# First self attention of a six-layer decoder kernel: eight batches in turn, or one chain of steps over all heads

## The chip, the cores and the metric

The kernel runs on one core of a Trainium2 chip, as one program. The metric is the device time in microseconds of one execution. TensorE is the matrix engine, VectorE and ScalarE read its results in PSUM, POOL (GpSimd) works on SBUF, and SyncE issues the transfers. Each engine takes its own instructions in program order and waits on semaphores.

## What is computed

A decoder of six layers over x of 8 batches x 256 tokens x 512, each followed by an addition and a layer normalization. Only the first, a causal self attention with 16 heads of width 128, is touched:

```python
q = (x @ Wq.T).reshape(b, n, H, D)              # H = 16, D = 128
kv = x @ Wkv.T                                  # one key part, one value part
kv_head = x @ Wkvh.T                            # one factor per head for k and v
g = x @ Wg.T
log_f_cumsum = cumsum([0, log_sigmoid(g)])[:-1]
kv_head = cumsum(kv_head * exp(log_f_cumsum))   # both over the tokens
k, v = kp x kh per head, vp x vh per head
q, k = rope(q), rope(k)
p = softmax(causal(q k^T / sqrt(D)))
x = layernorm(x + (p v) @ Wout.T)
```

## The kernel before

Float32 accuracy is kept by splitting: every operand of a product is a float16 high part and a float16 rest, and `three` (L114 to L116) issues three matmuls for one product. ScalarE rounds a PSUM bank to the high part, VectorE subtracts it from the bank for the rest; the pair is called hi and lo in the code.

`attn0` (from L316) loads and splits the weights, then goes through the eight batches one after the other. For each batch it first makes everything and then runs the heads:

- **x**: turned by TensorE (`turn_x`, L248) near the end of the batch before; `x_high` L255 on ScalarE, `x_low` L263 on VectorE.
- **Keys and values**: 24 matmuls of width 256 into the two S banks; ScalarE copies the values (L555), VectorE forms their rest and the rotated key (L631 to L636).
- **Gates**: 24 matmuls of width 256 into an O bank; ScalarE Abs, Exp, Ln (L558 to L562), VectorE two scans (L644, L648), between them ScalarE's Exp (L564). Their result is turned (L480) and copied (L673): one factor per token and head.
- **Queries**: eight products j of 12 matmuls of width 512 in the P banks. VectorE multiplies each with the rotation tables (L663, L664, L666), waits for itself and sets a semaphore by a small memset (L670), POOL adds the two parts (L421), TensorE turns four blocks (`turn`, L442), ScalarE and VectorE split them (L569, L623).
- **Keys per head**: POOL multiplies the rotated key with the factors (L411), eight times, TensorE turns (L442), ScalarE and VectorE split (L577, L623).
- **Heads**: a chain of 21 steps i. TensorE: scores of head i in one of two S banks (8 matmuls, the last of each half adds the mask, L503), turn of the probabilities (P) of head i-2, PV of head i-3 in one of two O banks, output product of head i-5 into the two P banks, which gather it over all heads. VectorE: row maxima (L690, L691), reciprocal (L698), rest of P (L704), rest of O (L711). ScalarE: P hi (L596), the exponentials (L585, L587, each with a read of the sum), O hi (L602). POOL weighs P with the reciprocals (L429, L431).
- **End**: VectorE adds x to the two output tiles (L285), measures (L288 to L291), POOL takes the root (L306), VectorE normalizes (L297).

PSUM has eight banks: two each of S, T (turned blocks), O and P. The order of the work is the program order of each engine's block; semaphores are counted per batch through `Counter` and `after`.

Of the kernel before, what the change touches and what calls it, by code (L numbers as in the profile page):

```python
# [7 lines left out]
F32 = mybir.dt.float32  # L8
F16 = mybir.dt.float16
# [7 lines left out]
P = 128  # L17
# [63 lines left out]
class Scope:  # L81
# [8 lines left out]
    def __exit__(self, *a):  # L90

        with self.nc.Block() as block:
# [223 lines left out]
def attn0(nc, G, W):  # L316
# [4 lines left out]
    NS = 2  # L321
    NPB = 3
    with Scope(nc, "a0", G.low) as sc:
# [10 lines left out]
        xT = [sc.sb(f"xT{i}", [P, KE, N], F16) for i in range(2)]  # L334
# [3 lines left out]
        v = [sc.sb(f"v{i}", [P, NT, D], F16) for i in range(2)]  # L338
        rope_q = sc.sb("rope_q", [P, 2, NT, D], F32)
        rope_k = sc.sb("rope_k", [P, 2, NT, D], F32)  # L340
        q_cos = sc.sb("q_cos", [P, 1, E], F32)
        q_sin = sc.sb("q_sin", [P, 1, E], F32)
        q_rot = sc.sb("q_rot", [P, 2, E], F32)
        k_part = sc.sb("k_part", [P, 2, D], F32)
        k_rot = sc.sb("k_rot", [P, NT, D], F32)
        kh_rows = sc.sb("kh_rows", [P, 1, H * D], F32)
# [5 lines left out]
        kvh_t = sc.sb("kvh_t", [P, NT, 2 * H], F32)  # L352
# [6 lines left out]
        NG = 8 + 8 + H  # L359
        G_Q, G_K, G_P = 0, 8, 16  # L360
        s = Names()
        x_counters(sc, s)
        s.t_ready = sc.counter("t_ready", NG)
        s.t_hi = sc.counter("t_hi", NG)
        s.t_lo = sc.counter("t_lo", NG)
        s.pr_ready = sc.counter("pr_ready", 2 + 8)
        s.pr_free = sc.counter("pr_free", 2 + 8)
        s.v_hi = sc.counter("v_hi", NT)
        s.gates_ready = sc.counter("gates_ready", 1)
        s.g_ln = sc.counter("g_ln", 3)  # L370
        s.g_sum = sc.counter("g_sum", 1)
        s.g_exp = sc.counter("g_exp", 1)
        s.kvh_ready = sc.counter("kvh_ready", 1)
        s.kvh_turned = sc.counter("kvh_turned", 1)
        s.kvh_t_ready = sc.counter("kvh_t_ready", 1)
        s.k_rot_ready = sc.counter("k_rot_ready", NT)
        s.kh_ready = sc.counter("kh_ready", 8)
        s.q_parts = sc.counter("q_parts", 8)
        s.q_ready = sc.counter("q_ready", 8)
        s.s_ready = sc.counter("s_ready", H)  # L380
        s.m_ready = sc.counter("m_ready", H)
        s.e_ready = sc.counter("e_ready", H)
        s.i_ready = sc.counter("i_ready", H)
        s.p_ready = sc.counter("p_ready", H)
        s.o_ready = sc.counter("o_ready", H)
        s.o_hi = sc.counter("o_hi", H)
        s.o_lo = sc.counter("o_lo", H)
        s.y_ready = sc.counter("y_ready", NT)
        s.chain = sc.counter("chain", NT * 1 + 2 + NT * LN_STEPS)
        ln_counters(sc, s)  # L390
        consts = sc.sem("consts")
        SB, Y = G.psS, G.psP

        with nc.Block() as block:
# [6 lines left out]
            @block.gpsimd  # L401
            def _(pool):
                for b in range(B):
                    def head_keys(j):

                        n, c = divmod(j, QC)
                        after(pool, s.kvh_t_ready, b, 1)
                        after(pool, s.k_rot_ready, b, n + 1)
                        if n:
                            after(pool, s.t_ready, b, G_K + c + 1)  # L410
                        pool.tensor_tensor(  # L411
                            kh_rows[:, 0, c * E:(c + 1) * E].rearrange("p (h d) -> p h d", h=HC),
                            k_rot[:, n:n + 1, :].broadcast_to([P, HC, D]),
                            kvh_t[:, n, c * HC:(c + 1) * HC].rearrange("p (h a) -> p h a", a=1)
                            .broadcast_to([P, HC, D]), ALU.mult).then_inc(s.kh_ready.handle, 1)

                    for j in range(8):
                        after(pool, s.q_parts, b, j + 1)
                        if j >= 2:
                            after(pool, s.t_ready, b, G_Q + j - 1)  # L420
                        pool.tensor_tensor(q_rot[:, j % 2, :], q_cos[:, 0, :], q_sin[:, 0, :], ALU.add)\  # L421
                            .then_inc(s.q_ready.handle, 1)
                        if j >= 5:
                            head_keys(j - 5)
                    for j in range(3, 8):
                        head_keys(j)
                    for h in range(H):
                        after(pool, s.i_ready, b, h + 1)
                        pool.tensor_tensor(prob[:, h % NPB, 0, 0:P], prob[:, h % NPB, 0, 0:P],  # L429
                                           inv[:, h % NPB, 0:1].broadcast_to([P, P]), ALU.mult)  # L430
                        pool.tensor_tensor(prob[:, h % NPB, 1, :], prob[:, h % NPB, 1, :],  # L431
                                           inv[:, h % NPB, 1:2].broadcast_to([P, N]), ALU.mult)\
                            .then_inc(s.p_ready.handle, 1)
                    for n in range(NT):
                        rstd_on_pool(pool, s, b, n, G)

            @block.tensor
            def _(pe):
                def turn(b, g, blocks):
                    after(pe, s.t_lo, b, g - 1)  # L440
                    for out, src in blocks:
                        last = pe.transpose(out, src, G.ident[:, :])  # L442
                    last.then_inc(s.t_ready.handle, 1)

                turn_x(pe, 0, s, G, G.psS)
                for b in range(B):
                    after(pe, s.x_lo, b, NT)
                    for n in range(NT):
                        for k in range(KE):
                            last = three(pe, G.psS[n][:, 0:2 * D], xT[0][:, k, n * P:(n + 1) * P],  # L450
                                         xT[1][:, k, n * P:(n + 1) * P], wkv[0][:, k, :], wkv[1][:, k, :],
                                         k == 0, k == KE - 1)
                        last.then_inc(s.pr_ready.handle, 1)
                    for i in range(2):
                        for k in range(KE):
                            last = three(pe, G.psO[0][0:2 * H, i * N:(i + 1) * N],
                                         wgh[0][:, k, i * 2 * H:(i + 1) * 2 * H], wgh[1][:, k, i * 2 * H:(i + 1) * 2 * H],
                                         xT[0][:, k, :], xT[1][:, k, :], k == 0, k == KE - 1)
                    last.then_inc(s.gates_ready.handle, 1)

                    def turn_q(j):
                        after(pe, s.q_ready, b, j + 1)
                        turn(b, G_Q + j, [(G.psT[j % 2][:, i * P:(i + 1) * P], q_rot[:, j % 2, i * P:(i + 1) * P])
                                          for i in range(HC)])

                    for j in range(8):
                        n, c = divmod(j, QC)
                        if j == 0:
                            after(pe, s.x_done, b, 0)
                        after(pe, s.pr_free, b, j + 1)  # L470
                        if j == 4:
                            after(pe, s.kvh_ready, b, 1)
                        for k in range(KE):
                            last = three(pe, G.psP[j % 2][:, :], xT[0][:, k, n * P:(n + 1) * P],
                                         xT[1][:, k, n * P:(n + 1) * P], wq[0][:, k, c * E:(c + 1) * E],
                                         wq[1][:, k, c * E:(c + 1) * E], k == 0, k == KE - 1)
                        last.then_inc(s.pr_ready.handle, 1)
                        if j == 4:
                            for n2 in range(NT):
                                last = pe.transpose(G.psO[1][:, n2 * 2 * H:(n2 + 1) * 2 * H],  # L480
                                                    kvh[:, n2 * P:(n2 + 1) * P], G.ident[0:2 * H, 0:2 * H])
                            last.then_inc(s.kvh_turned.handle, 1)
                        if j >= 2:
                            turn_q(j - 2)
                    turn_q(6)
                    turn_q(7)
                    for n in range(NT):
                        for c in range(QC):
# [5 lines left out]
                    def scores(h):  # L494
                        if h >= NS:
                            after(pe, s.e_ready, b, h - NS + 1)
# [2094 lines left out]
```

## Time and profile before

| What | Value |
|---|---|
| Time, median of 3 runs | 3481.63 us (3477.75 to 3481.8) |
| Profiled execution | 3481.1 us |
| Its span | 3479.1 us |
| PE busy in the span | 2910.5 us, 84% |
| VectorE, ScalarE, POOL busy | 2108.0, 1764.8, 1404.9 us |
| First self attention | 48.0 to 819.9 us of the span |

Times within the span are counted from its start. A busy PE includes matmuls that overlap in the pipeline, so the time of a group of matmuls is best read as the distance between starts. The granted clock is the share of 2.4 GHz: 1.00 is 2.4 GHz, 0.50 is 1.2 GHz, and a value between is a mean over time. A timeline's row gives start, duration, engine, line, operation, what it writes and reads, and how many consecutive ones are merged; the brackets tell how long the engine had been idle and what released it.

### The profile page before, as it was taken

Reading aid. Unit: us, or ns where it says so; the run is one execution under the profiler, and the core shown is the slowest. Engines: PE = TensorE matmul, PEld = TensorE weight load, DVE = VectorE, ACT = ScalarE, POOL = GpSimd, SP = SyncE. Lnnn points to the kernel's source line nnn. Section 1 sums busy time; section 2 is a strip of 40 time slices with the busy share of each in tenths; the row PEclk is TensorE's granted clock in tenths of the full one; section 3 lists DMA queues with packets and bytes.
Section 4 is the critical chain, followed back from the end, with each engine's and each line's share of the span. In section 5 each row is a group of like instructions: output and inputs, shape, how many; then the busy total and the mean of one; then the engine's idle time right before and its main releaser. Section 6 shows DMA issues by size and latency. Waiting matters only on the chain. (4 is left out here: it accounts for less than half of the span.)

```text
span 3479.1 us, 64422 instructions
## 1 busy us (share of the span) xinstructions
PE 2910.5 (84%) x24866; PEld 2050.9 (59%) x24866; DVE 2108.0 (61%) x4574; ACT 1764.8 (51%) x3865; POOL 1404.9 (40%) x1537
## 2 busy tenths in 40 slices
PE   4989889894888886699999978887999999975777
PEld 2566555552566664577777756665766666752333
DVE  4666666665677774555555446665555555555887
ACT  3444444443788886433333246664444444454775
POOL 1333343332587886244444424442122222213453
PEclk9988998987899997799999999998999999997898
DMA  4000000001000000300000001102011110022000
GB/s 159 1 1 1 1 1 1 1 1 64 1 2 2 2 2 20 135 1 13 1 1 1 1 34 38 32 2 67 2 37 37 37 37 1 1 73 67 12 19 25
DMA packets 41189, 81.49 MB, mean 23 GB/s; under 512 B 5683, under 2 KB 9781, under 8 KB 40758
## 3 DMA queue, kind: packets, MB, share of 16 engines
q1 hardware_dynamic: 40886, 77.38, 6.5%
q8 instruction: 199, 3.26, 0.4%
q14 instruction: 104, 0.85, 0.1%
HBM read 73.18 MB, written 4.19 MB: 22 GB/s over the span
## 5 line engine op out<-in xcount | busy, mean ns | idle before, releaser
L960 POOL TENSOR_TENSOR c_pT<-c_prob,c_pT 128x512 f16<-128x512 f32 x256 | 293.4, 1159 | 106.4 <-ACT c_pT L917 105.7
L1813 POOL TENSOR_TENSOR c_prob<-c_prob,c_inv 128x512 f32<-128x512 f32 x128 | 133.5, 1043 | 310.6 <-DVE c_inv L2037 310.6
L960 POOL TENSOR_TENSOR a_pT<-a_prob,a_pT 128x384 f16<-128x384 f32 x128 | 120.6, 945 | 189.5 <-ACT a_pT L917 189.1
L1151 ACT ACTIVATE c_prob<-psT 128x512 f32<-128x512 f32 x256 | 155.8, 609 | 70.0 <-PE psT L1082 56.0
L1232 DVE TENSOR_REDUCE c_peak<-psS 128x2 f32<-128x512 f32 x256 | 169.8, 683 | 20.7 <-PE psS L1063 17.4
L917 ACT CAST c_pT<-c_prob 128x512 f16<-128x512 f32 x256 | 159.7, 624 | 0.0
L421 POOL TENSOR_TENSOR a_q_rot<-a_q_cos,a_q_sin 128x512 f32<-128x512 f32 x64 | 81.0, 1265 | 192.0 <-DVE a_q_sin L666 192.0
L429 POOL TENSOR_TENSOR a_prob<-a_prob,a_inv 128x128 f32<-128x128 f32 x128 | 51.1, 399 | 256.7 <-DVE a_inv L698 256.7
L596 ACT ACTIVATE a_pT<-psT,a_kvh_t 128x256 f16<-128x256 f32 (+1 forms) x256 | 93.6, 416 | 105.0 <-PE psT L442 105.0
L1961 ACT CAST c_pT<-psT 128x512 f16<-128x512 f32 x128 | 74.8, 584 | 140.0 <-PE psT L1825 140.0
L1953 ACT ACTIVATE c_prob<-psS,c_negmax 128x256 f32<-128x256 f32 x256 | 119.2, 474 | 44.8 <-DVE c_negmax L2030 41.2
L1489 POOL TENSOR_TENSOR f_ch<-f_h,f_c 128x256 f32<-128x256 f32 x88 | 76.1, 865 | 147.6 <-DVE f_h L1682 147.6
L114 PE MATMUL psP<-a_wq,a_xT 128*128 128x512 f16 x320 | 121.4, 379 | 13.1 <-DVE junk L670 10.3
L306 POOL TENSOR_TENSOR ln_rstd<-ln_ve,minus_half 128x1 f32<-128x1 f32 x48 | 31.9, 665 | 247.2 <-DVE ln_ve L291 247.2
L704 DVE SCALAR_TENSOR_TENSOR a_pT<-psT,a_kvh_t,a_pT 128x256 f16<-128x256 f32 (+1 forms) x256 | 95.1, 413 | 59.6 <-ACT a_pT L596 59.4
L2165 POOL TENSOR_TENSOR f_hg<-f_h,f_g 128x512 f32<-128x512 f32 x64 | 81.4, 1271 | 119.2 <-DVE f_h L2370 119.2
L2211 PE MATMUL psS<-f_wq,f_xq 128*128 128x512 f16 x256 | 81.6, 477 | 56.1 <-DVE f_h L2370 49.7
L1687 DVE TENSOR_TENSOR f_chs<-f_ch,f_chs 128x768 f16<-128x768 f32 x88 | 107.3, 1220 | 33.0 <-ACT f_chs L1625 32.4
L1063 PE MATMUL psS<-c_kS,c_qS 128*128 128x256 f16 x512 | 105.2, 290 | 24.0 <-DVE c_peak L1232 21.3
L115 PE MATMUL psP<-a_wq,a_xT 128*128 128x512 f16 x320 | 121.3, 379 | 0.0
L116 PE MATMUL psP<-a_wq,a_xT 128*128 128x512 f16 x320 | 121.3, 379 | 0.0
L569 ACT CAST a_qT<-psT 128x512 f16<-128x512 f32 x64 | 36.7, 586 | 163.4 <-PE psT L442 163.4
(580 smaller groups left out, 11456.7 us busy)
## 6 DMA issues: line engine op xcount, KB each, us to landing
c_feed<-in_L_ffn_w1T SPq DMA_DIRECT2D x16, 512.0 KB, 3.6
c_feed<-in_L_ffn_w2T SPq DMA_DIRECT2D x16, 512.0 KB, 3.6
f_stage<-in_f_up_gateT SPq DMA_DIRECT2D x16, 352.0 KB, 8.0
x_all<-in_x SPq DMA_DIRECT2D x1, 4096.0 KB, 14.1
a_stage<-in_L_attn_WqT SPq DMA_DIRECT2D x8, 512.0 KB, 7.6
a_stage<-in_L_attn_WoutT SPq DMA_DIRECT2D x8, 512.0 KB, 10.0
a_feed<-in_L_xattn_Wq SPq DMA_DIRECT2D x8, 512.0 KB, 3.7
c_feed<-in_L_xattn_Wo SPq DMA_DIRECT2D x8, 512.0 KB, 3.9
```

The costliest lines, as they stand in the source:

```text
L114: pe.matmul(out, a_hi, b_hi, start=first, stop=False, skip_group_check=True)
L115: pe.matmul(out, a_hi, b_lo, start=False, stop=False, skip_group_check=True)
L116: return pe.matmul(out, a_lo, b_hi, start=False, stop=last, skip_group_check=True)
L704: last = dve.scalar_tensor_tensor(pT[1][:, r, m, m * P:N], T[:, m * N + m * P:(m + 1) * N], kvh_t[:, m, H + h:H + h + 1], pT[0][:, r, m, m ...
L917: copy(pT[0][:, c % NPH, :], prob[:, c % NPX, :]).then_inc(p_high(c)[0], 1)
L960: pool.tensor_tensor(pT[1][:, c % NPH, :], prob[:, c % NPX, :], pT[0][:, c % NPH, :], ALU.subtract)\
L1063: last = pe.matmul(S[:, first:first + w], qS[:, b % 2, h // HB, n * P:(n + 1) * P], kS[:, b % 2, k_of(h), 0:w], start=True, stop=not causa ...
L1151: act.activation(prob[:, c % NPX, :], ST[c % 2][:, 0:EW], ACT.Exp).then_inc(s.e_done, 1)
L1232: dve.tensor_reduce(peak[:, h, :], S, X_AXIS, ALU.max).then_inc(s.m_done, 1)
L1687: dve.tensor_tensor(chs[1][:, t % 2, :, :], ch[:, t % 2, :, :], chs[0][:, t % 2, :, :], ALU.subtract).then_inc(s.ch_lo.handle, 1)
L1813: pool.tensor_tensor(prob[:, h % NPB, :, :], prob[:, h % NPB, :, :], inv[:, h % NPB, :].rearrange("p (n a) -> p n a", a=1).broadcast_to([P ...
L1953: last = act.activation(prob[:, r, n, :], S[:, n * N:(n + 1) * N], ACT.Exp, bias=negmax[:, r, n:n + 1], accum_out=sums[:, r, n:n + 1])
```

## The change

The loop over batches with its two parts is replaced by one loop over steps t from -14 to 135. Step t begins head t of all 128 heads (batch t // 16). What the next batch needs is made in steps given relative to its first head, so that it lies within the steps of this one:

- x at -14 (both tiles), keys and values at -12, gates at -10, their turn at -6; ScalarE's and VectorE's later parts of the gates one to three steps after -10.
- Query products at -7, -5, -3, -1, 1, 3, 5, 7, each turned two steps later; keys turned at -4, -2, ..., 10. So queries and their turns fall on odd steps, the keys' turns on even ones. Both are made head group by head group (four heads), for both token tiles.
- Output products come in pairs, of heads t-6 and t-5, in even steps.
- Layer normalization: the sum with x 20 steps after the batch's first head, measuring at 21, normalizing at 22.
- Bank use: S and O now have one bank each (`S`, `O`); the other two (`XB`) take x, kv, gates, the gates' turn and the query products in turn. The turn banks T alternate over all turns (k, q and P). The P banks hold the output products only.
- xT, v, kvh_t, k_rot double in size (by batch parity), k_part holds both tiles; the gates are copied out of PSUM once (`g_raw`). The two memsets after the rotations (L639, L670) go. Semaphores count over the whole part.

The diff, cut to its core (the first loop over t is POOL's, the second TensorE's):

```diff
-    NS = 2
     NPB = 3
+    AT_X, AT_KV, AT_GATES, AT_KVH = (-14, -14), -12, -10, -6
+    AT_Q = (-7, -5, -3, -1, 1, 3, 5, 7)
+    AT_K = (-4, -2, 0, 2, 4, 6, 8, 10)
+    TURN_Q, TURN_P, PV, WO, NORM = 2, 2, 3, 5, 21
+    FIRST, LAST = AT_X[0], (B - 1) * H + NORM + 3
...
-        SB, Y = G.psS, G.psP
+        S, O, Y = G.psS[0], G.psO[0], G.psP
+        TB, XB = G.psT, [G.psS[1], G.psO[1]]
...
+                for t in range(FIRST, LAST):
+                    for b, j in due(t, AT_K, -1):
+                        head_keys(b, j)
+                    if head(t, 1) is not None:
+                        weigh(head(t, 1))
+                    for b, j in due(t, AT_Q):
+                        add_q(b, j)
+                    for b, n in due(t, (NORM, NORM)):
+                        rstd(b, n)
...
+                def turn(key, blocks):
+                    no = turn_no[key]
+                    if no >= 2:
+                        pe.wait_ge(s.t_lo, no - 1)
...
+                def scores(a):
+                    b, h = divmod(a, H)
+                    if a:
+                        pe.wait_ge(s.e_ready, a)
...
+                for t in range(FIRST, LAST):
+                    if head(t, 0) is not None:
+                        scores(head(t, 0))
+                    for b, j in due(t, AT_K):
+                        turn_k(b, j)
+                    for b, j in due(t, AT_Q, TURN_Q):
+                        turn_q(b, j)
+                    for lag in (WO + 1, WO):
+                        if t % 2 == 0 and head(t, lag) is not None:
+                            project(head(t, lag))
+                    if head(t, TURN_P) is not None:
+                        turn_p(head(t, TURN_P))
+                    for b, n in due(t, AT_X):
+                        turn_x(b, n)
+                    for b, _ in due(t, (AT_KV,)):
+                        keys_values(b)
+                    for b, _ in due(t, (AT_GATES,)):
+                        gates(b)
+                    for b, _ in due(t, (AT_KVH,)):
+                        turn_kvh(b)
+                    for b, j in due(t, AT_Q):
+                        queries(b, j)
+                    if head(t, PV) is not None:
+                        pv(head(t, PV))
```

ScalarE's order in a step: hi of the keys' and of the queries' turn, exponentials of head t, the gates' second Exp, P hi, x hi, value copy, the gates' Abs, Exp and Ln, O hi of head t-3. VectorE's: row maxima of head t, lo of the keys' and the queries' turn, reciprocal of head t-1, the gates' scans, P lo of head t-2, the sums with x, x lo, the key's rotation, the gates' copies, the rotation of the queries, O lo of head t-3, measuring, normalizing.

## Rows read from the trace of the kernel before

**Rows 1.** Busy windows of batch 3: window, length, busy us by engine, PEclk, DMA share, GB/s

```profile
372.00:385.00 13.00, 8.41 (x42) 6.43 (x43) 6.04 (x9) 5.17 (x9) 5.95 (x6) 0.63 0.00 1
335.00:431.00 96.00, 86.54 (x588) 57.31 (x586) 60.84 (x176) 44.10 (x139) 35.06 (x50) 0.91 0.00 1
```

**Rows 2.** The tile a_xT on VectorE: durations, first and last start

```profile
L263 DVE TENSOR_TENSOR a_xT<-psS,a_xT x16: 680/686/692, 48.0 to 717.3; 128x512 f16<-128x512 f32 x16
```

**Rows 3.** Timeline: first scores, and the last batch's normalization on VectorE

```profile
96.46 0.29 PE L114 MATMUL psS<-a_kT,a_qT 128*128 128x128 f16 x1 [1.40 <-DVE a_kT L623]
...
814.89 0.69 DVE L285 TENSOR_TENSOR ln_r<-psP,x_all 128x512 f32<-128x512 f32 x1 [2.41 <-PE psP L116]
...
819.35 0.55 DVE L297 TENSOR_SCALAR x_all<-ln_r,ln_mv,ln_rstd 128x512 f32<-128x512 f32 x1 [0.44 <-POOL ln_rstd L306]
```

**Rows 4.** Timeline of TensorE over one head of batch 3, first matmul of each group

```profile
400.20 0.22 PE L114 MATMUL psS<-a_kT,a_qT 128*128 128x128 f16 x1
...
400.81 0.50 PE L442 MATMUL psT<-ident,a_prob 128*128 128x128 f32 x3
...
401.14 0.27 PE L114 MATMUL psO<-a_pT,a_v 128*128 128x256 f16 x1
...
401.64 0.38 PE L114 MATMUL psP<-a_wo,a_qT 128*128 128x512 f16 x1
...
402.93 0.22 PE L114 MATMUL psS<-a_kT,a_qT 128*128 128x128 f16 x1
```

**Rows 5.** Timeline of TensorE in batch 7: kv, gates, turn of queries, query product

```profile
720.20 0.27 PE L114 MATMUL psS<-a_wkv,a_xT 128*128 128x256 f16 x1
...
722.91 0.28 PE L114 MATMUL psO<-a_xT,a_wgh 128*32 128x256 f16 x1
...
735.20 0.60 PE L442 MATMUL psT<-ident,a_q_rot 128*128 128x128 f32 x4
735.64 0.38 PE L114 MATMUL psP<-a_wq,a_xT 128*128 128x512 f16 x1
...
738.23 0.60 PE L442 MATMUL psT<-ident,a_q_rot 128*128 128x128 f32 x4
```

**Rows 6.** Timeline of VectorE, then of ScalarE, over the same head

```profile
400.44 0.42 DVE L711 TENSOR_TENSOR a_qT<-psO,a_qT 128x256 f16<-128x256 f32 x1 [0.32 <-ACT a_qT L602]
401.00 0.29 DVE L690 TENSOR_REDUCE a_negmax<-psS 128x1 f32<-128x128 f32 x1
401.21 0.41 DVE L691 TENSOR_REDUCE a_negmax<-psS 128x1 f32<-128x256 f32 x1
...
402.11 0.74 DVE L704 SCALAR_TENSOR_TENSOR a_pT<-psT,a_kvh_t,a_pT 128x256 f16<-128x256 f32 x2 [0.41 <-ACT a_pT L596]
...
401.34 0.73 ACT L596 ACTIVATE a_pT<-psT,a_kvh_t 128x256 f16<-128x256 f32 x2 [0.94 <-PE psT L442]
401.96 0.37 ACT L585 ACTIVATE a_prob<-psS,a_negmax 128x128 f32<-128x128 f32 x1
...
402.66 0.22 ACT L587 ACTIVATION_READ_ACCUMULATOR a_prob<-psS,a_negmax 128x1 f32 x1
```

**Rows 7.** Timeline of VectorE and POOL in a rotation of queries

```profile
366.35 0.69 DVE L663 TENSOR_TENSOR a_q_cos<-psP,a_rope_q 128x512 f32<-128x512 f32 x1 [0.72 <-POOL a_q_rot L421]
...
367.74 0.69 DVE L623 TENSOR_TENSOR a_qT<-psT,a_qT 128x512 f16<-128x512 f32 x1
...
364.98 1.26 POOL L421 TENSOR_TENSOR a_q_rot<-a_q_cos,a_q_sin 128x512 f32<-128x512 f32 x1 [1.89 <-DVE a_q_sin L666]
```

**Rows 8.** Timeline in the gates: last scan of batch 0, table load in batch 3

```profile
62.18 0.68 DVE L648 TENSOR_TENSOR_SCAN a_kvh<-ones,a_g_fac 32x256 f32<-32x256 f32 x1
...
344.70 1.28 ACT L562 ACT_TABLE_LOAD   x1
```

**Rows 9.** Busy windows of two later layers: columns as in rows 1

```profile
1110.00:1160.00 50.00, 42.48 (x573) 30.49 (x570) 35.89 (x71) 40.62 (x74) 41.46 (x40) 1.00 0.01 2
3274.00:3291.00 17.00, 13.73 (x72) 6.44 (x72) 14.65 (x31) 12.50 (x19) 9.05 (x9) 0.90 0.09 32
```

More of the change, by code:

```diff
@@ new lines, in attn0, with due, head, turns @@
+        s.chain = sc.sem("chain")
+        consts = sc.sem("consts")
+        def due(t, places, shift=0):
+            out = []
+            for i, at in enumerate(places):
+                b, rest = divmod(t - shift - at, H)
+                if rest == 0 and 0 <= b < B:
+                    out.append((b, i))
+            return out
+        def head(t, lag):
+            return t - lag if 0 <= t - lag < B * H else None
+        def turns(t):
+            out = [("k", b, i) for b, i in due(t, AT_K)] + [("q", b, i) for b, i in due(t, AT_Q, TURN_Q)]
+            if head(t, TURN_P) is not None:
+                out.append(("p", *divmod(head(t, TURN_P), H)))
+            return out
@@ L453, in _, with gates @@
-                        last.then_inc(s.pr_ready.handle, 1)
+                            last = three(pe, bank(key)[:, n * 2 * D:(n + 1) * 2 * D], xT[0][:, r, k, rows],
+                                         xT[1][:, r, k, rows], wkv[0][:, k, :], wkv[1][:, k, :], k == 0, k == KE - 1)
+                    last.then_inc(s.x_ready, 1)
+                def gates(b):
+                    key, r = ("gates", b, 0), b % 2
+                    make_free(key)
                     for i in range(2):
+                        at = slice(i * 2 * H, (i + 1) * 2 * H)
@@ L466, in _ @@
[L466 to L484, printed above, removed]
@@ L535, in _ @@
[L535 to L547 removed]
+                            last = three(pe, bank(key)[0:2 * H, i * N:(i + 1) * N], wgh[0][:, k, at], wgh[1][:, k, at],
+                                         xT[0][:, r, k, :], xT[1][:, r, k, :], k == 0, k == KE - 1)
@@ new lines, in gates, with turn_kvh, queries @@
+                    last.then_inc(s.x_ready, 1)
+                def turn_kvh(b):
+                    key = ("kvh", b, 0)
+                    pe.wait_ge(s.kvh_ready, b + 1)
+                    make_free(key)
+                    for n in range(NT):
+                        last = pe.transpose(bank(key)[:, n * 2 * H:(n + 1) * 2 * H], kvh[:, n * P:(n + 1) * P],
+                                            G.ident[0:2 * H, 0:2 * H])
+                    last.then_inc(s.x_ready, 1)
+                def queries(b, j):
+                    key, r = ("q", b, j), b % 2
+                    c, n = divmod(j, NT)
+                    rows, cols = slice(n * P, (n + 1) * P), slice(c * E, (c + 1) * E)
+                    make_free(key)
+                    for k in range(KE):
+                        last = three(pe, bank(key)[:, :], xT[0][:, r, k, rows], xT[1][:, r, k, rows],
+                                     wq[0][:, k, cols], wq[1][:, k, cols], k == 0, k == KE - 1)
+                    last.then_inc(s.x_ready, 1)
@@ new lines, in turned, with hi_p @@
+                def turned(key, out):
+                    act.wait_ge(s.t_ready, turn_no[key] + 1)
+                    act.copy(out, turn_bank(key)[:, :].rearrange("p (k t) -> p k t", k=HC)).then_inc(s.t_hi, 1)
+                def hi_p(a):
+                    b, h = divmod(a, H)
+                    T = turn_bank(("p", b, h))
+                    act.wait_ge(s.t_ready, turn_no["p", b, h] + 1)
+                    if a >= 2:
+                        act.wait_ge(s.o_ready, a - 1)
+                    for m in range(NT):
+                        last = act.mul(pT[0][:, a % 2, m, m * P:N], T[:, m * N + m * P:(m + 1) * N],
+                                       kvh_t[:, b % 2, m, H + h:H + h + 1])
+                    last.then_inc(s.t_hi, 1)
```

606 lines of the change are left out of this document (309 added, 297 removed).

## The prediction

> **What bounds it now.** I first read the page (TensorE's share and the clock row), then the busy windows of one batch, then the timeline of each engine in that batch. L263, twice per batch, starts first at 48.0 and last at 717.3; less the 0.6 between the two of a batch that is 95.5 us per batch, and the whole part runs from 48.0 to 819.9 us [rows 2, 3]. I read batch 3 in detail; the others have the same pattern. Inside it the head loop is bound by TensorE alone: from 400.20 to 402.93 a head takes 2.73 us with no gap, of which scores 0.61, turn of the probabilities 0.33, PV 0.50, output product 1.29 [rows 4]. What isn't bound by TensorE lies around it. From 372 to 385 us, where the last queries and all keys are turned, PE is busy 8.4 of 13 us at a granted clock of 0.63; the batch's mean clock is 0.91 [rows 1]. There each turn waits for ScalarE's rounding and VectorE's subtraction of an earlier one. So the batch's time is the work of TensorE, plus hand-over gaps, plus work at the 1.2 GHz level after them.
>
> **TensorE's own work per batch at 2.4 GHz.** 16 heads x 2.73 = 43.7 [rows 4]. A query product lasts 738.23 - 735.64 = 2.59, x8 = 20.7; a turn of four blocks 735.64 - 735.20 = 0.44, x16 for queries and keys = 7.0, and 2 x 0.44 = 0.9 for x; keys and values 722.91 - 720.20 = 2.7, the gates about the same (24 matmuls of the same width), 2.6 [rows 5]. The gates' turn I take at 0.2, as half of one such turn. Sum 77.7 us against 95.5. The change adds or removes no matmul, so 17.8 us per batch is the most it can take from a batch's middle.
>
> **What replaces it: a step.** After the change a step holds one head and one slice of the next batch's work. Odd steps: scores 0.61, turn of queries 0.44, turn of P 0.33, query product 2.59, PV 0.50 = 4.47. Even steps: 0.61, turn of keys 0.44, two output products 2.58, turn of P 0.33, PV 0.50 = 4.46. The pair is 8.9 us, x8 = 71.4, and x, kv, gates and their turn (6.4) are laid on even steps.
>
> **Does the single score bank hold it up?** Two S banks become one, so scores(t+1) wait for both exponentials of t. Row maxima: 401.00 to 401.62 = 0.62. Exponentials: 401.96 to 402.88 = 0.92. From the end of the scores' issue (400.81 [rows 4]) to the reduction is 0.2. So 0.61 + 0.2 + 0.62 + 0.05 + 0.92 + 0.05 = 2.45 us [rows 6], under the 4.5 of a step: cost nothing, covered by 2 us of other matmuls. The single O bank needs ScalarE's copy and VectorE's 0.42 [rows 6] before the next PV, a step later: nothing. If the cover goes (last steps, no queries), the loop shows; see below.
>
> **Does VectorE hold it up?** In an odd step it issues row maxima 0.55, subtraction for the queries 0.6, reciprocal 0.15, subtraction for P 0.7, three rotation products 1.3, subtraction for O 0.35 = 3.65; in an even one 2.35. (Rotation: 366.35 to 367.74 is 1.39 with the wait on itself that the change drops; the subtraction after it takes 0.69 and overlaps its follower by 0.1 [rows 7].) The rotation waits for the query product, 4.1 us into the step, so it and the O subtraction end 1.3 us into the next. That next is even and light; its row maxima start 0.5 us late, its exponentials end 2.9 us in, before 4.46. It catches up. POOL has three operations in an odd step, the longest the queries' sum with 1.26 [rows 7]: under 3.8 of 4.5, covered; its results are wanted one or two steps later.
>
> **A wait that appears.** The turn banks alternate q/k, p, q/k, p, so P always lands in the same bank: turn of P waits for VectorE's subtraction of the P before. An even step turns P at 3.63, the odd one at 1.05 of the next, 1.88 later. The chain is 0.53 to ScalarE (400.81 to 401.34 [rows 4, 6]), 0.73, 0.04, 0.74, 0.15 back (an estimate, as the 0.19 from TensorE to VectorE above) = 2.19: a stall of 0.3 at each even-to-odd edge, except where x, kv or gates stand between. Four such a batch: 1.2, less 0.2 where the gates' turn covers.
>
> **The gates' step.** ScalarE does Abs, Exp, a table load of 1.28 [rows 8], Ln = 2.5 us ahead of the O copy, and loads Exp's table again, 1.28, ahead of the next exponentials. Walking the queues step by step: scores after it start 1.2 late, the next 0.25, then the turn of P 0.8. In all 2.3. The sums, measuring and normalizing (814.89 to 819.90, 5.0 us for two tiles [rows 3]), moved to steps 4 to 6 of the next batch, lie on two steps that kv and gates stretch to 7 us: I take nothing; if that cover fails it is up to 5 us a batch. Two fewer sequencing memsets per product cost or give nothing, being off PE.
> Stalls together 3.4, so a batch takes 77.7 + 3.4 = 81.1 us instead of 95.5.
>
> **The edges.** Start: the first L263 stays at 48.0, as rope's DMA releases it. The gate scan ends at 62.86 as now [rows 8]; the first rotation and POOL's sum end at 65.4; then three rounds of turn 0.44, product 2.59, 0.2, rotation 1.3, POOL 1.26 = 5.8, of which the last stops at the product: scores(0) at about 80. In these rounds PE is half idle, so part will be at 1.2 GHz: 0 to 8 us, I take 4, from the 0.63 of [rows 1]: 84, where now it is 96.5 [rows 3]. Between scores(0) and scores(127): 8 x 77.7 = 621.6, less 19 done before (x, kv, gates, four products, five turns), less 10.7 left after (six output products, three PVs and turns) = 592; stalls 7 x 3.4 = 24, 2 in the first steps without output products, and in the last batch 8: from step 123 a pair has only 5.4 us of matmuls, while the chain P subtraction, O subtraction, row maxima, exponentials makes it 7.1. Scores(127) at 84 + 592 + 34 = 710. After it: 4.0 us of matmuls until P(126) is turned, 2.2 to the turn of P(127), 0.8 with the PV between, two output products 2.6, PV(127) 0.5, two more 2.6, 0.2, and the last normalization 5.0: 18. End at 728 against 819.9: 92 us less.
>
> **Sum.** The profiled execution took 3481.1 us (span 3479.1), 0.5 under the median of 3481.63. 3481 - 92 = 3389 us. Unknown terms: stalls from 0 (all covered) to 10 us per batch (all of the normalizing and the gates' chain exposed); clock at the start 0 to 8. This gives 3351 to 3440.
>
> **Rival 1: the clock does not rise.** Many short gaps may keep dropping the clock. Windows differ: from 3274 to 3291 with PE busy 13.7 of 17 it was 0.90; from 1110 to 1160, busy 42.5 of 50 with many gaps, it was 1.00 [rows 9]. The new steps have gaps of at most 1.3 us and PE is at work about 95%, nearer to the latter. If the mean stays at 0.91 [rows 1], 592 becomes 651: 3389 + 59 = 3448.
> The Trainium skill, in "TensorE: Matmul & The Clock Gate", section "A second HAM failure mode: psum-queue depth-cycling", says that a kernel of 512-wide matmuls cycling through PSUM banks idles briefly between groups often enough for the clock to swing between its two levels. This change alternates banks in just that way. By that rule it is the 3448 of this rival; the window from 1110 in [rows 9] speaks against it.
>
> **Rival 2: VectorE's lateness doesn't die out.** Measuring in step 5 (about 2 of the 5.0 us above, on 3.65) and the scans in steps 7 and 9 (0.41 + 0.68 [rows 8]) lengthen VectorE to 5.7 and 4.8 against 4.5. If each of the pairs loses 1 us: 7 x 8 = 56: 3445. Against: even steps have 2 us of slack.
>
> **Rival 3: slower.** One ring closes through all engines: turn of P, query product, rotation, O subtraction, row maxima, exponentials, ScalarE's P copy, P subtraction, turn of P: 0.33 + 2.59 + 0.2 + 1.3 + 0.35 + 0.62 + 0.05 + 0.92 + 0.73 + 0.04 + 0.74 + 0.15 = 8.0 per pair, under the 9.1 with stalls. It decides from 9.1 on and eats the gain at (95.5 - 6.4 - 2.3) / 8 = 10.9, that is 2.9 us more in some ten hand-overs. At 11.5 a batch is 100.7: 7 x 5.2 = 36 more, less 12 at the start: 3505. Against: L263's sixteen durations, the same kind of operation, lie between 0.680 and 0.692 us [rows 2].
>
> **Rival 4: no overlap in fact.** In-order queues could keep the making apart from the heads; then 3481. Against: the order within a step puts query product between P turn and PV.
>
> **Chances.** Forecast 0.69, rival 1 0.12, rival 2 0.12, rival 3 0.04, rival 4 0.03. The forecast's low end with some stall left is 3355; up to rivals 1 and 2, 3450. A change under 0.2% (7 us) couldn't be told from none. Faster 0.93, same 0.03, slower 0.04.
>
> **What would show it.** Right: L263's period near 81 us; PE without the hole around the key turns; clock 1.0 from about 90 us to the end of the part; waits of P's turn on VectorE of about 0.3 us; one stall near 1.2 us per batch on exponentials, after the gates; first scores near 84. Wrong: period above 88, the clock row alternating within the part (rival 1), PE waiting for exponentials in every step (rivals 2, 3), or TensorE's work per step not 4.5.

## Result and profile after

| What | Before | Changed |
|---|---|---|
| Time, median | 3479.69 us (3472.82 to 3481.8, 4 runs) | 3386.19 us (3379.68 to 3387.53, 4 runs) |
| Ratio, 95% interval | | 0.9734 (0.9718 to 0.9749) |
| Profiled execution, span | 3481.1, 3479.1 us | 3379.68, 3377.7 us |
| First self attention ends | 819.9 us | 724.5 us |
| One batch, start to start | 95.5 us | 80.75 us |
| PE busy | 2910.5 us, 84% | 2857.4 us, 85% |

The change is 2.7% faster. The first self attention ends 95.4 us earlier. The rest of the span, from that end on, is 2653.2 us after 2659.2; in the profiled executions of this study it lies between 2651.4 and 2659.7 whatever the kernel, so those 6 us are scatter, not an effect. All distances below are taken inside the first self attention, where two profiles of the same kernel agree within 0.1 us per batch.

Busy windows of the changed kernel, columns as in [rows 1] (window, length, busy us of PE, PEld, VectorE, ScalarE, POOL, granted clock, DMA share, GB/s):

```profile
335.00:431.00 96.00, 94.35 (x704) 63.80 (x703) 67.91 (x194) 52.79 (x162) 40.90 (x58) 1.00 0.00 1
281.40:362.15 80.75, 79.09 (x586) 53.24 (x587) 56.76 (x161) 45.03 (x138) 35.73 (x51) 1.00 0.01 1
52.00:84.00 32.00, 22.20 (x113) 12.39 (x112) 11.92 (x26) 7.48 (x12) 6.77 (x6) 0.84 0.00 1
84.00:706.90 622.90, 603.30 (x4484) 405.93 (x4481) 432.08 (x1232) 346.59 (x1066) 274.96 (x388) 1.00 0.01 1
706.90:724.50 17.60, 12.02 (x79) 6.72 (x76) 9.68 (x29) 4.91 (x17) 3.27 (x6) 1.00 0.00 1
```

The first row is the same stretch as in [rows 1]: PE is busy 94.35 of 96 us in place of 86.54, and the granted clock is 1.00, the 2.4 GHz level, in place of 0.91. The second row is exactly one batch: 79.09 of 80.75 us busy. The fourth shows that the clock held its upper level for the 623 us from the first scores to the last.

What PE still waits for, whole part (engine, bank and line, releaser: us in total, times, longest):

```profile
PE psS L116 <- ACT a_prob L653: 10.8, 13, 1.9
PE psT L490 <- POOL a_q_rot L444: 7.0, 3, 2.3
PE psT L490 <- DVE a_pT L733: 4.3, 9, 0.5
PE psS L116 <- DVE a_xT L820: 2.9, 1, 2.9
PE psO L553 <- DVE a_kvh L811: 2.8, 1, 2.8
PE psO L116 <- DVE a_qT L740: 2.1, 4, 0.6
PE psT L490 <- POOL a_prob L465: 0.2, 1, 0.2
```

They sum to 30.1 us. Three of them (7.0, 2.9, 2.8) lie before the first scores, once, and not once per batch; the longest behind the first scores, 1.9, is at the second head. The same view of before sums to 75.5 us and is led by key turns on VectorE and query turns on POOL, both gone inside the pipeline:

```profile
PE psT L442 <- DVE a_kT L623: 17.4, 24, 1.0
PE psT L442 <- POOL a_q_rot L421: 15.4, 8, 2.0
```

The stalls of one batch, in the timeline of PE (start, duration, ..., and in brackets the idle time and its releaser):

```profile
281.40 0.23 PE L116 MATMUL psS<-a_kT,a_qT 128*128 128x128 f16 x1 [0.67 <-ACT a_prob L653]
...
287.71 0.52 PE L490 MATMUL psT<-ident,a_prob 128*128 128x128 f32 x3 [0.54 <-DVE a_pT L733]
...
304.88 0.22 PE L116 MATMUL psS<-a_kT,a_qT 128*128 128x128 f16 x1
...
305.49 0.61 PE L490 MATMUL psT<-ident,a_q_rot 128*128 128x128 f32 x4
306.24 0.52 PE L490 MATMUL psT<-ident,a_prob 128*128 128x128 f32 x3
306.60 0.38 PE L116 MATMUL psS<-a_wq,a_xT 128*128 128x512 f16 x1
```

The first is the wait for the exponentials two steps after the gates, the second the wait of P's turn a step on. The last three rows are an edge from an even to an odd step: the queries' turn begins at 305.49 and needs 0.44, but P's turn begins at 306.24, so 0.31 us are lost. The view prints no bracket there, since the previous matmul is still in the pipeline; a row's start minus the one before it finds such holes.

The distance from the start of one head's scores to the next, over one batch from 205.2 us on (worked out from the timeline of PE):

```
5.21 4.81 4.46 4.47 4.79 4.47 4.80 4.46 4.80 5.34 4.46 7.09 4.46 7.30 5.29 4.55   sum 80.76
```

A step without anything extra is 4.46. The first 4.81 holds the gates' turn, 5.34 the turn of x, 7.09 keys and values, 7.30 the gates. The three odd steps of 4.79 to 4.80 hold an edge with its 0.33. What follows the gates, 5.29, 4.55 and 5.21, is 1.67 over three plain steps; the brackets show 0.67 and 0.54 of it. So TensorE's own work is 16 x 4.46 + 0.35 + 0.88 + 2.63 + 2.84 = 78.06, and 1.0 + 1.67 = 2.67 are stalls.

### The profile page after: what moved, and what is told of

Its sections match the earlier page's. It is cut to its first block and busy times, and to the rows that moved or that the text cites. A ratio compares the mean times of both kernels' runs of the same rounds, so it can differ in the third digit from the quotient of the medians.

```text
span 3377.7 us, 64410 instructions
## 1 busy us (share of the span) xinstructions
PE 2857.4 (85%) x24866; PEld 2022.3 (60%) x24866; DVE 2074.5 (61%) x4462; ACT 1771.8 (52%) x3857; POOL 1409.7 (42%) x1537
## 5 line engine op out<-in xcount | busy, mean ns | idle before, releaser
L444 POOL TENSOR_TENSOR a_q_rot<-a_q_cos,a_q_sin 128x512 f32<-128x512 f32 x64 | 81.1, 1267 | 193.1 <-DVE a_q_sin L752 193.1
L1194 PE MATMUL psT<-c_qS,c_kS 128*128 128x256 f16 x512 | 105.2, 290 | 15.4 <-ACT c_prob L1263 14.4
L1721 ACT ACTIVATE f_sil<-psS 128x256 f32<-128x256 f32 x48 | 18.4, 383 | 180.2 <-PE psS L118 180.2
L2142 DVE TENSOR_REDUCE c_negmax<-psS 128x2 f32<-128x512 f32 x128 | 87.8, 686 | 40.6 <-PE psS L1987 40.6
L2153 DVE TENSOR_TENSOR c_pT<-psT,c_pT 128x512 f16<-128x512 f32 x128 | 87.5, 684 | 37.6 <-ACT c_pT L2073 36.8
L116 PE MATMUL psO<-c_v_ones,c_pT 128*128 128x17 f16 x1024 | 104.3, 173 | 2.6 <-POOL c_pT L1072 2.6
```

Source lines behind the costliest of these rows:

```text
L116: pe.matmul(out, a_hi, b_hi, start=first, stop=False, skip_group_check=True)
L1194: last = pe.matmul(out, kS[:, b % 2, k_of(h), m * P:(m + 1) * P], qS[:, b % 2, h // HB, q0:N], start=True, stop=not causal, skip_group_che ...
```

## Experiments

All are made against the changed kernel unless said otherwise. "Period" is the distance between equal events of two consecutive batches in the profile. The theory under test (A) is the prediction's: TensorE's own work sets the pace inside the pipeline, with small stalls at the edges and after the gates. The rivals are the clock, the ring of hand-overs, and VectorE.

**The changed kernel again.** No edit.

> The changed kernel once more, unaltered, as the reference of this group. The first profile showed the part's end at 724.5 us, a period of 80.75 us per batch, and a total of 3386 us in the median. Both theories expect 3380 to 3388 us and the same period to 0.1 us.

3382.54 us (3379.39 to 3383.78, 5 runs), ratio 0.9724 (0.9711 to 0.9737), period 80.75, end of the part at 725.2. It is the base for what follows.

**P's turn ahead of the output products.** In the even steps:

```diff
+                    if head(t, TURN_P) is not None:
+                        turn_p(head(t, TURN_P))
                     for lag in (WO + 1, WO):
                         if t % 2 == 0 and head(t, lag) is not None:
                             project(head(t, lag))
-                    if head(t, TURN_P) is not None:
-                        turn_p(head(t, TURN_P))
```

> In even steps TensorE turns the probabilities before the two output products instead of after them. Theory A (the 0.31 us gap before the turn of P in odd steps comes from VectorE's subtraction of the P before, late because the even step turns P late): the gap vanishes at its four places per batch, period 80.75 - 1.2 = 79.5 us, total 8 to 10 us less. It leaves the two waits after the gates. Theory B (these gaps are TensorE's own change between turns and cost the same anywhere): period 80.7 to 80.8, total unchanged.

3369.73 us (3368.94 to 3378.03), ratio 0.9691 (0.9678 to 0.9704); period 79.74; end of the part 716.4. The edge in its timeline:

```profile
304.95 0.61 PE L490 MATMUL psT<-ident,a_q_rot 128*128 128x128 f32 x4
305.40 0.49 PE L490 MATMUL psT<-ident,a_prob 128*128 128x128 f32 x3
305.73 0.38 PE L116 MATMUL psS<-a_wq,a_xT 128*128 128x512 f16 x1
```

P's turn follows the queries' after 0.45, without the hole. The three steps of 4.80 became 4.46, and the three after the gates still exceed plain ones by 1.67. So the stall at the edges is the turn of P coming too soon for the chain through its one bank, as the prediction had it, and costs 1.0 us per batch. Within the part the profile gives 8.8 us (725.2 to 716.4); the median fell by 12.8, and what lies between is not explained.

**The gates ahead, on TensorE and on ScalarE.** TensorE's gate products move ahead of the output products, ScalarE's Abs, Exp and Ln ahead of the copy of P:

```diff
+                    for b, _ in due(t, (AT_GATES,)):
+                        gates(b)
                     for lag in (WO + 1, WO):
...
-                    for b, _ in due(t, (AT_GATES,)):
-                        gates(b)
```

> In the gates' step TensorE makes the gates before the output products, and ScalarE does Abs, Exp and Ln before its P copy. Theory A (the wait on the exponentials, 0.68 us idle, and the wait on P's subtraction, 0.54 us idle, once per batch after the gates, come from ScalarE's chain with two table loads starting at the end of the step): both vanish or shrink to under 0.2, period 79.2 to 79.8 us, total 7 to 12 us less. Theory B (VectorE's normalization and copies in the same step are what is late): period unchanged within 0.3 us, total within 3 us. A new wait is possible: P's copy queued behind Ln, seen by PV a step later.

3382.64 us (3381.6 to 3384.2), ratio 0.9724 (0.9711 to 0.9737): no gain, against 7 to 12 us expected. Period 80.90. The wait for the exponentials is gone, and another is in its place. Timelines of PE, ScalarE and VectorE:

```profile
278.61 0.52 PE L490 MATMUL psT<-ident,a_prob 128*128 128x128 f32 x3 [1.01 <-DVE a_pT L733]
...
275.37 1.28 ACT L684 ACT_TABLE_LOAD   x1
276.67 0.41 ACT L684 ACTIVATE a_g_log<-a_g_abs 32x256 f32<-32x256 f32 x1
276.99 0.70 ACT L642 ACTIVATE a_pT<-psT,a_kvh_t 128x256 f16<-128x256 f32 x2
...
277.72 0.74 DVE L733 SCALAR_TENSOR_TENSOR a_pT<-psT,a_kvh_t,a_pT 128x256 f16<-128x256 f32 x2 [3.35 <-ACT a_pT L642]
```

Now the copy of P stands behind the table load and Ln, VectorE's subtraction behind the copy, and the next turn of P (1.01) behind that. A table load moved along its queue is paid by whoever is queued behind it.

**P first, both gate moves, and the start.** As the two before together; before the first scores, the queries are also made ahead of the earlier ones' turn:

```diff
+                    if t < 0:
+                        for b, j in due(t, AT_Q):
+                            queries(b, j)
                     for b, j in due(t, AT_Q, TURN_Q):
                         turn_q(b, j)
```

> Turn of P before the output products, gates early (between the two), and in the steps before the first head the query product issued before the turn of the product before it. Theory A: the period falls by the sum of both single moves, to 78 to 78.4 us, near the 77.7 of TensorE's own work; the first scores come at 77 instead of 84 us, as the product of 2.6 us no longer waits for POOL's sum. Total 22 to 28 us under the changed kernel, about 3360. Theory B (the ring through the engines, not TensorE, sets the step): period not under 80, total within 8 us but for the start.

3365.63 us (3362.76 to 3370.89), ratio 0.9679 (0.9666 to 0.9693); period 79.87 against an expected 78 to 78.4, first row maxima at 79.9 instead of 85.1 to 86.6 in the runs before it, end of the part at 709.7. The period is that of P first alone, so the gates' part gave nothing here either; the start gave 5 to 7 us.

**Only TensorE's part of the gates ahead.** As the run before, but ScalarE's three functions stay behind the copy of P.

> The turn of the weights goes ahead of the x products, TensorE's gate work goes ahead of the output products while ScalarE's three gate functions stay behind the copy of P, and before the first scores the queries are made one step earlier. If the three gains stand apart from each other, the period of a batch falls from 80.75 to about 78.4 us (79.74 with the early turn of P, less .85 for the wait of the gates' step that the scores see, less about .5 for the copy of P no longer behind the logarithm), first scores at about 78 us, the part ends at about 703 us and the total is 3354 to 3362 us. If the logarithm's table loads hold up the exponentials wherever TensorE's part of the gates stands (rival), the gates' part gives nothing: a period of 79.7 to 79.9 and a total of 3364 to 3368 us.

3364.62 us (3360.6 to 3365.16), ratio 0.9674 (0.9661 to 0.9687); period 78.88, end of the part at 707.6. The wait for the exponentials is gone and P's turn waits 0.33:

```profile
276.84 0.52 PE L490 MATMUL psT<-ident,a_prob 128*128 128x128 f32 x3 [0.33 <-DVE a_pT L737]
```

So the gates' stall falls by 0.86 per batch against P first alone, as expected; the further 0.5 that I had taken for the copy of P did not come. This is read from the period: the ratios of P first alone, of the three moves and of this run have intervals that overlap, so their total times don't tell them apart. The total is 3364.6 against an expected 3354 to 3362, a miss by 2.6. In the profiled execution 2.9 us stand in one place. After a wait of 3.1 us at the second head, which the two runs with the same start have too, only this one shows the clock falling (window, length, PE busy, clock; first this kernel, then the next):

```profile
82.00:89.00 7.00, 6.53 (x24) 0.54 0.00 0
```

```profile
82.00:89.00 7.00, 6.33 (x53) 1.00 0.00 0
```

The step after it takes 6.59 us there and 3.65 in the other two.

**Two banks each for S and O in the last seven heads.** As the run before; where no more queries are made, their two banks are free.

```diff
+        Y, TWO = G.psP, B * H - 7
...
+        def S_of(a):
+            return G.psS[a % 2 if a >= TWO else 0]
...
                     if a:
-                        pe.wait_ge(s.e_ready, a)
+                        pe.wait_ge(s.e_ready, a - 1 if a > TWO else a)
```

> As the run before it, and in the last seven heads of the last batch, where nothing is made for a next batch, scores and outputs alternate between two banks each. The waits of that stretch in the run of the changed kernel (1.34, .70, .50, .81, .80, .65 us) should go: 4 to 6 us less than the run before it, the part's end moved by as much, the period of a batch unchanged. If the waits there are set by VectorE and ScalarE and not by banks (rival), it is within 1.5 us of the run before it.

3360.77 us (3353.12 to 3365.08), ratio 0.9667 (0.9651 to 0.9682), the fastest kernel of the study by its median, though its interval overlaps the last one's. The end of the part is at 702.6, 5.1 earlier, which looks like a hit. It isn't: 1.1 of the 5.1 is that the first scores begin earlier, and 2.9 the clock of the second step above; the last seven distances between scores sum to 24.7 in place of 25.3, and from the last scores to the end are 17.3 in place of 17.8. The second banks gave 1.1 us. What PE waits for there, in the run before it and in this one:

```profile
PE psS L116 <- ACT a_prob L657: 2.6, 4, 0.8
PE psT L490 <- POOL a_prob L465: 1.0, 1, 1.0
```

```profile
PE psT L496 <- POOL a_prob L471: 2.2, 3, 1.2
PE psT L496 <- DVE a_pT L749: 1.1, 2, 0.9
PE psS L116 <- ACT a_prob L669: 0.3, 1, 0.3
```

The wait moved from scores to the turn of P, most of it behind POOL's weighing (0.40 and 0.61 us) of the probabilities. The rival holds: without work of a next batch, the chain of the other engines sets the last heads, not the banks.

**More work for TensorE.** Two more matmuls of 256 columns ahead of each PV, into the same bank, overwritten by the true product's start:

```diff
+                    for _ in range(2):
+                        pe.matmul(O[:, 0:N], v[0][:, b % 2, 0, :], pT[0][:, a % 2, 0, :], start=True, stop=False,
+                                  skip_group_check=True)
```

> The changed kernel with two more matmuls of 256 columns (.11 us each) ahead of each output product, overwritten by it, 128 times over. If TensorE is what sets the pace inside the pipeline (theory), nearly all of 128 x .22 = 28 us shows: a period of about 84 us against 80.75 and a total of 3408 to 3416 us. If the round of scores, exponentials, turn and outputs sets it, and TensorE waits inside it (rival), the extra work falls into the waits: a period below 82 and a total below 3396 us.

3398.65 us (3396.12 to 3401.81, 4 runs), ratio 0.9775 (0.976 to 0.979); period 82.93. Neither number was hit: 2.17 of the 3.52 us per batch show. The distances between scores say why; the second line is this run, at the same heads as the first, the changed kernel:

```
5.21 4.81 4.46 4.47 4.79 4.47 4.80 4.46 4.80 5.34 4.46 7.09 4.46 7.30 5.29 4.55   sum 80.76
5.27 5.03 4.68 4.68 4.81 4.68 4.80 4.68 4.80 5.55 4.68 7.30 4.69 7.51 5.08 4.69   sum 82.93
```

Every step without a wait grew by 0.21 to 0.23, the whole of the two matmuls. The steps with a wait at the edge kept their 4.80, and the step that waits for the exponentials became shorter, 5.29 to 5.08: part of that wait sat in the work of the step before. So TensorE sets the length of ten of the 16 steps, and a chain through the other engines takes part in the rest. My figure for theory A forgot that added work fills the stalls first.

**No logarithm.** This leaves out the logarithm of the gates (a second Exp stands in its place), and with it both table loads:

```diff
-                        act.activation(g_log[:, :], g_abs[:, :], ACT.Ln, bias=1.0).then_inc(s.g_act, 1)
+                        act.activation(g_log[:, :], g_abs[:, :], ACT.Exp, scale=-1.0).then_inc(s.g_act, 1)
```

> The changed kernel with the gates' Ln replaced by Exp, which leaves the logarithm of the gates out and so drops both table loads of 1.28 us per batch. Theory A (the table loads on ScalarE cause the two waits after the gates): both waits vanish, period 80.75 - 1.5 = 79.2 us, total 10 to 13 us less. Theory B (the waits come from VectorE's scans and normalization): period unchanged within 0.3 us.

3371.46 us (3362.37 to 3377.26, 4 runs), ratio 0.9697 (0.9674 to 0.972); period 79.47. The wait for the exponentials is gone, that of P's turn is 0.19 instead of 0.54. The two loads of 1.28 us cost 1.28 us per batch: half of their time was covered. With this the steps after the gates exceed plain ones by 0.38 in place of 1.67.

**Two score banks, one bank for the making.** The prediction put the single S bank at nothing. Here S has two banks and x, keys, gates and queries share one:

```diff
-        S, O, Y = G.psS[0], G.psO[0], G.psP
-        TB, XB = G.psT, [G.psS[1], G.psO[1]]
+        SB, O, Y = G.psS, G.psO[0], G.psP
+        TB, XB = G.psT, [G.psO[1]]
```

> The changed kernel with both S banks for the scores; x, kv, gates and query products then share one bank instead of two. Theory A (a single score bank costs nothing in the middle): the waits on exponentials go (0.85 per batch after the gates, some 5 us in the last batch), but x's second tile waits for its first one, about 2 us per batch; period 81.5 to 83 us, total 3386 to 3402. Theory B (the single score bank holds up every step): period under 79 us despite the shared bank, total under 3375.

3396.66 us (3388.79 to 3401.97, 4 runs), ratio 0.9766 (0.9745 to 0.9786); period 82.73. Scores no longer wait in mid-batch, but the second tile of x and P's turn do:

```profile
PE psO L523 <- DVE a_xT L821: 16.6, 8, 3.2
PE psT L490 <- DVE a_pT L734: 10.8, 8, 1.4
```

The distances between scores say where the 2 us are: the step with x takes 7.32 in place of 5.34, and the three steps after the gates sum to 15.04, as with one score bank (15.05). So in mid-batch a second score bank only moves the wait to P's turn and gives nothing, as the prediction had it, and the second making bank is worth 2 us per batch.

**The same steps without overlap.** Thirty steps per batch instead of 16. No head runs while x, keys, values, gates and the first four queries of a batch are made; the other queries and most keys are still made among the batch's own heads:

```diff
-    FIRST, LAST = AT_X[0], (B - 1) * H + NORM + 3
+    PER = 30
+    FIRST, LAST = AT_X[0], (B - 1) * PER + NORM + 3
...
-                b, rest = divmod(t - shift - at, H)
+                b, rest = divmod(t - shift - at, PER)
```

> The changed kernel with 30 steps per batch instead of 16: heads in steps 0 to 15, and x, kv, gates and the first half of the queries of the next batch in steps 16 to 29, where no head runs. All work, banks, buffers and orders within a step are as in the changed kernel; only the overlap of the two parts goes. Theory A (the gain is the overlap): a batch takes 90 to 98 us again, PE has holes of 2 to 3 us at POOL's query sums, the granted clock falls in them; total 3450 to 3500 us. Theory B (the gain comes from the rest: fewer semaphores and memsets, one copy for both tiles, head groups in another order): total 3386 to 3400.

3581.55 us (3572.67 to 3583.13, 4 runs), ratio 1.0295 (1.0276 to 1.0314): slower than before, and outside the range I had given. Busy windows (PE, clock) of a stretch of heads and of a stretch of making, and the largest waits:

```profile
194.00:245.00 51.00, 43.95 (x340) 1.00 0.00 1
245.00:302.00 57.00, 40.67 (x241) 0.88 0.00 1
```

```profile
PE psT L492 <- POOL a_q_rot L446: 55.0, 24, 2.4
PE psS L116 <- ACT a_prob L655: 52.3, 48, 1.9
PE psO L116 <- DVE a_qT L742: 22.6, 32, 1.4
PE psS L555 <- DVE a_kvh L813: 22.3, 4, 5.6
PE psO L555 <- DVE a_kvh L813: 19.6, 4, 5.6
```

A batch takes 109.2 us against 95.5 before and 80.75. Waits at the single S and O banks, rare under cover, come to 75 us where it is gone (52.3 + 22.6), the turn of queries waits 55 us for rotation and sum, and the turn of the gates 42 us for the scans. That second banks would save the 75 us is not shown: in the run with two banks for the last heads they gave 1.1 us and moved the wait. What is shown is that the gain needs the overlap; this order of steps without it loses 3%.

**Before, with the clock held up.** The kernel of before with three added matmuls of 512 columns into a free bank ahead of each turn of keys and of the last two of queries, results unused:

```diff
+                            for _ in range(3):
+                                pe.matmul(G.psO[1][:, :], xT[0][:, 0, 0:P], wq[0][:, 0, 0:E], start=True, stop=True,
+                                          skip_group_check=True)
```

> The kernel before with three dummy matmuls of width 512 (0.65 us at 2.4 GHz) into the unused O bank ahead of each of the eight key turns and of the last two query turns; nothing else. It splits the old batch's 95.5 - 77.7 = 17.8 us into clock and holes. If it is mostly the clock: the granted clock goes to 0.98 or more, a batch takes 82 to 86 us, total 3385 to 3410. If it is mostly the holes between hand-overs (my theory): clock to 0.98, but a batch still 90 to 93 us, total 3440 to 3465. If the dummies lengthen the chain more than the clock gives: no change or slower.

3456.33 us (3455.92 to 3457.42, 4 runs), ratio 0.9943 (0.9926 to 0.9959); about 93.1 us per batch. Its windows, columns as in [rows 1]:

```profile
372.00:385.00 13.00, 8.82 (x83) 6.39 (x81) 8.13 (x25) 8.11 (x31) 3.83 (x8) 1.00 0.00 1
335.00:428.00 93.00, 86.44 (x618) 55.85 (x617) 61.19 (x175) 44.03 (x138) 35.06 (x51) 1.00 0.00 1
```

The clock is 1.00 where it was 0.63, and a batch gains 2.4 us of the 14.75. That is what the clock gives back less what the added matmuls cost, and the two can't be told apart here. The other 12 us need the holes filled: this window still has 6.6 us of idle time, with the added matmuls counted as busy, where the changed kernel has 1.65 of 96. By an estimate the 30 added matmuls, 0.215 us apart, fill another 6.5 us, so 13 of the 93 us are holes in the kernel's own work at the 2.4 GHz level.

## Why the prediction was right

The forecast was 3389 us, the median is 3386.19, inside the range; the mechanism was the forecast's own, none of the rivals'. Point by point:

- **TensorE's work per batch, 77.7.** Measured 78.06. A plain step is 4.46, as worked out (4.47 and 4.46), the turn of x 0.88 (0.9), keys and values 2.63 (2.7), the gates 2.84 (2.6), their turn 0.35 (0.2). The run without the logarithm gives the same: 79.47 less 1.03 at edges and 0.38.
- **Stalls, 3.4.** Measured 2.67. The edges were put at four times 0.3 less 0.2; they are three times 0.33, the fourth hidden behind the gates' turn, and P's turn moved ahead removes them. The gates' step was put at 1.2, 0.25 and 0.8, together 2.3, and takes 0.83, 0.09 and 0.75, together 1.67: the same three places, the first of them put nearly half too high. That the table loads and the gates' place cause it is shown by the run without the logarithm (0.38 left) and by the one with TensorE's gate products ahead (0.81 left).
- **Slips in the sums.** TensorE's terms as listed sum to 77.8, not 77.7, and the stalls to 3.3, not 3.4; the two cancel in 81.1. The 10.7 us left after the last scores needs four PVs, where three are named.
- **The items at nothing.** Single S bank: under cover no wait except after the gates, and with two banks that one only moves. The normalization of the batch before: the step with its measuring, between 7.09 and 7.30, is 4.46, so nothing.
- **Start, 84.** The first scores begin at 83.66, but by other parts than given. Timeline of PE:

```profile
64.48 1.12 PE L490 MATMUL psT<-ident,a_q_rot 128*128 128x128 f32 x4 [2.28 <-POOL a_q_rot L444]
65.39 0.63 PE L116 MATMUL psS<-a_wq,a_xT 128*128 128x512 f16 x1
65.81 0.63 PE L117 MATMUL psS<-a_wq,a_xT 128*128 128x512 f16 x1
...
72.93 1.12 PE L490 MATMUL psT<-ident,a_q_rot 128*128 128x128 f32 x4 [2.35 <-POOL a_q_rot L444]
...
80.58 0.66 PE L490 MATMUL psT<-ident,a_q_rot 128*128 128x128 f32 x4 [2.35 <-POOL a_q_rot L444]
...
83.66 0.22 PE L116 MATMUL psS<-a_kT,a_qT 128*128 128x128 f16 x1
```

```profile
65.00:68.50 3.50, 3.50 (x11) 0.50 0.02 5
68.50:73.00 4.50, 2.15 (x11) 0.88 0.00 0
73.00:76.00 3.00, 3.00 (x10) 0.50 0.00 0
76.00:80.50 4.50, 2.23 (x12) 0.97 0.00 0
```

  Rounds take 8.45 and 7.65 us, not 5.8: after the first two waits on the sum the turn and the next product begin at the 1.2 GHz level (clock 0.50, 0.43 us from matmul to matmul instead of 0.215) and the clock rises within the product. After the third wait, as long, it is at the upper level. At 5.8 a round the scores would have begun at 79.2. Of the 4.5 between, 4.1 are turns and products at the lower level (5.50 and 4.70 us in place of 3.03), where I took 4 out of 0 to 8, from the 0.63 of another stretch: that this came out so close is luck. The first turn, at 64.5 in place of 65.4, offsets the rest.
- **End.** Last scores at 706.84 (710), 17.6 us behind them (18). The last two pairs of heads take 7.11 each (7.1). The wait of the last heads was blamed on VectorE's chain; with second banks POOL's weighing sets most of it.
- **Sum.** The part came out 95.4 us shorter, against 92. From the first to the last scores it took 623.2, against 626: seven times the 0.7 of stalls that were overpriced, less seven times the 0.36 of work that was underpriced, is about 2.4 of these 2.8. The profiled time, 3379.68, is a further 6 shorter by the scatter of the later layers.
- **Rival 1.** The clock was 1.00 over 622.9 us. The rule of the Trainium skill cited with it (TensorE: Matmul & The Clock Gate, "A second HAM failure mode: psum-queue depth-cycling") would have kept the swing and given 3448. This trace disagrees: 512-wide matmuls cycling through banks, with waits of up to 0.7 us inside the pipeline, 1.3 in the last heads and 1.9 at the second head, kept the upper level. The clock fell in the start and in one profile at the second head, at waits of 2.3 us and more, but not at every such wait.
- **Rivals 2, 3 and 4.** The light even step has the slack that was claimed: 4.46 where nothing waits. Rival 3 needed pairs of 10.9; pairs of plain steps take 8.9 to 9.3, those after the gates up to 10.0. Adding 3.52 us of work to TensorE showed 2.17, so these chains are close behind: they own the stalls, not the pace. Rival 4, no overlap in fact, is out with 94.35 of 96 us busy.

What stays open is why the clock fell at one wait of 3.1 us and not at two others like it, and how much of the 14.75 us is the clock's and how much the holes': the two aren't additive, and only one side was measured alone.

## What to carry to other kernels

Find the step's own length on the bounding engine first (here 4.46), then read distances between equal instructions and explain each surplus: that shows stalls that the brackets hide. Overlapping a maker and a user can pay for giving up double buffers, but test the layout without the overlap: here, with 30 steps per batch, it lost 3%. In an in-order queue, put what feeds the next hand-over ahead of what only fills (P's turn before output products: 1.0 us per batch for one moved line), and move a long instruction, such as a table load, only where nobody stands behind it.

## What the runs showed that was not expected

- The same start gave two clocks: around a wait of 3.1 us the granted clock was 0.54 in one profile and 1.00 in two others, 2.9 us apart. In the changed kernel it was 0.50 after two waits of 2.3 us and 1.00 after a third. Differences of 3 us between single profiles need this check first.
- Two table loads of 1.28 us cost 1.28 us per batch together, and moving them moved the cost to another wait: 0.67 and 0.54 became 1.01 and 0.42.
- Holding the clock near 1.00 with added matmuls made the kernel of before 0.6% faster although it gave TensorE more to do.
